# A third early chunk, the last batch's low halves between the two maxima, and a reordered hand-over from attention to the experts

## The reference, cut to what matters

```python
# x: 8 x 512 x 256, context: 8 x 1024 x 256, 8 heads of 64, 8 experts, d_ff 1024, top-2
x = x + tanh(g_xattn) * (softmax(q k^T * 64**-0.5) v @ Wo + bo)     # q from layernorm(x), k and v from context
h = layernorm(x).reshape(4096, 256)
probs = softmax(h @ router.T); topk_probs, selected = top_k(probs, 2)   # weights normalised to sum 1
# each expert takes at most capacity = 1280 (token, weight) pairs, heaviest first
# weights are normalised again per token over what was kept
pre, gate = h_e @ W1_e.T, h_e @ Wg_e.T
out[token] += kept_weight * ((pre * silu(gate)) @ W2_e.T)
x = x + tanh(g_ffn) * out
```

## Time and profile before

| | |
|---|---|
| median of 3 runs | 1765.65 us (1765.6 to 1765.99) |
| the profiled execution | 1766.5 us, its span 1764.8 us |
| busy share | PE 95%, DVE 72%, ACT 60%, POOL 39% |
| chain that ended last | PE 79%, DVE 9%, issue 4%, POOL 3%, ACT 2% |
| attention | to about 1085 us |
| hand-over (END, two early chunks) | about 1085 to 1149 us |
| regular chunks of the experts | 1149 us to the end |

### The profile page before, as it was taken

The page is one execution under the profiler, slowest core; times in us unless marked ns, Lnnn a source line. Parts: engine busy times, 40 slices in busy tenths (PEclk is TensorE's granted clock), DMA queues, the critical chain, the costliest instruction groups (busy, mean ns, idle before and its releaser), DMA issues.

```text
span 1764.8 us, 35399 instructions
## 1 busy us (share of the span) xinstructions
PE 1683.3 (95%) x13198; PEld 1534.2 (87%) x13198; DVE 1268.9 (72%) x2664; ACT 1055.9 (60%) x2233; POOL 688.4 (39%) x622
## 2 busy tenths in 40 slices
PE   6999999999999999999999987899999999999998
PEld 5778888888888888888888876899999999999998
DVE  6888888888888888888888876665465555645443
ACT  5767667667667667767767765354454444545443
POOL 3342444444444444444444335234232323333323
PEclk9999999999999999999999998999999999999999
DMA  4300210210210210210200223232331313131111
GB/s 123 122 25 1 109 49 26 110 48 26 110 48 25 111 48 25 112 47 25 112 35 25 112 82 104 72 101 41 102 103 31 102 31 102 34 99 31 30 30 25
DMA packets 60040, 114.40 MB, mean 65 GB/s; under 512 B 7032, under 2 KB 47992, under 8 KB 59264
## 3 DMA queue, kind: packets, MB, share of 16 engines
q1 hardware_dynamic: 43856, 93.50, 14.9%
q0 software_dynamic: 16048, 19.09, 6.1%
HBM read 88.67 MB, written 57.97 MB: 83 GB/s over the span
## 4 chain that ended last, share of the span: by engine, by line
PE 79%; DVE 9%; issue 4%; POOL 3%; ACT 2%; DMA 1%; POOLq 0%; DVEq 0%; SPq 0%
PE ffn L1020 11%; PE ffn L1022 11%; PE ffn L1021 11%; PE ring L1163 11%; PE turned L1057 11%; PE scores L1045 9%; DVE neg_max L1765 4%; PE ring L1020 4%; PE ring L1022 3%; PE ring L1021 3%; DVE pt_l L1542 2%; PE ring L1129 1%; PE ring L1131 1%; POOL lists L841 1%; POOL probs L866 1%
## 5 line engine op out<-in xcount | busy, mean ns | idle before, releaser
L866 POOL TENSOR_SCALAR probs<-probs,row_rec 128x1024 f32<-128x1024 f32 x256 | 285.4, 1128 | 477.3 <-DVE row_rec L1844 464.1
L1337 ACT ACTIVATE pt_h<-turned 128x512 fp32r<-128x512 f32 x512 | 280.1, 603 | 208.2 <-PE turned L1057 207.9
L1542 DVE TENSOR_TENSOR pt_l<-turned,pt_h 128x512 fp32r<-128x512 f32 x512 | 331.5, 681 | 6.7 <-ACT pt_h L1337 5.7
L1765 DVE TENSOR_REDUCE neg_max<-scores 128x1 f32<-128x1024 f32 x256 | 301.3, 1218 | 36.8 <-PE scores L1045 36.8
L1057 PE MATMUL turned<-ident,probs 128*128 128x128 f32 x2048 | 281.9, 279 | 31.6 <-DVE pt_l L1542 24.4
L1057 PEld LDWEIGHTS turned<-ident,probs 128*128 128x128 f32 x2048 | 223.3, 141 | 100.7 <-issue 72.0
L1393 ACT ACTIVATE probs<-scores,neg_max 128x1024 f32<-128x1024 f32 x256 | 285.4, 1117 | 10.4 <-DVE neg_max L1765 10.4
L1163 PE MATMUL ring<-pt_h,v_hl 128*128 128x256 f32 x1024 | 262.9, 294 | 0.2
L2059 DVE TENSOR_TENSOR act_f<-ffn,silu 128x256 f32<-128x256 f32 x288 | 122.2, 424 | 191.0 <-ACT silu L1489 184.9
L1489 ACT ACTIVATE silu<-ffn 128x256 f32<-128x256 f32 x288 | 110.7, 384 | 237.6 <-PE ffn L1022 225.1
L1163 PE MATMUL ring<-pt_l,v_hl 128*128 128x256 f32 x1024 | 252.3, 284 | 0.0
(11 more groups left out here) (239 smaller groups left out, 4073.7 us busy)
## 6 DMA issues: line engine op xcount, KB each, us to landing
lists<-pads SPq DMA_DIRECT2D x8, 4160.0 KB
w_raw<-w_t SPq DMA_DIRECT2D x14, 1024.0 KB, 6.3
e_rows<-lists SPq DMA_DIRECT2D x37, 260.0 KB
ctx_raw<-ctx_t SPq DMA_DIRECT2D x15, 512.0 KB, 3.7
wg_raw<-wg_t SPq DMA_DIRECT2D x7, 1024.0 KB
x_in<-x SPq DMA_DIRECT2D x8, 512.0 KB, 4.0
x_sum<-x SPq DMA_DIRECT2D x8, 512.0 KB, 3.9
out<-x_sum SPq DMA_DIRECT2D x8, 512.0 KB, 2.9
```

Of the source, the lines that this page charges most:

```text
L866: nc.gpsimd.tensor_scalar(probs[:, k, :], probs[:, k, :], row_rec[:, k:k + 1], 1.0, ALU.mult, ALU.mult).then_inc(scaled, 1)
L1337: return nc.scalar.activation(dst, src, ACT.Copy)
L1542: return nc.vector.tensor_tensor(dst, src, hi_part.bitcast(F32), ALU.subtract)
L1765: nc.vector.tensor_reduce(neg_max[:, k:k + 1], scores[:, n % 2, :].rearrange("p (a c) -> p a c", a=2), AX.XY, ALU.max, negate=True).then_i ...
```

## The change

1. `EARLY` is 3: expert 0's third chunk, too, is written out as an early chunk, with its result in `y_early`. An expert's chunks after the early ones are at least `LEAST_MORE` = 2, so expert 0 has at least five. Each early chunk transposes the next chunk's rows at its part 6, and takes the high and low halves of them at part 7.
2. `closing` has another order: END 0 and 1, the rows of chunk 0, END 2 and 3, then the early chunks with the other END steps behind named parts. The projections ("w", 1, 2) and ("w", 1, 3) are now behind part 0. The search is spread over parts 0 to 8 of early chunk 2.
3. In the last batch at steps 24 to 30 DVE takes the low halves of unit u - 2 between the maxima of u and u + 1. The reciprocals of the last two units are apart, and POOL scales each when it is there. "r" of batch 6 is at step 25, its DVE part after both maxima of step 26; POOL scatters two by two at steps 27 to 30.
4. ACT's six high pieces are at LAST 23, 25, 27, 29 and END 3, 4. POOL's low pieces, ten, are all at END 0, in the order 0, 2, 4, 6, 1, 3, 5, 7, 8, 9, behind its wait for the scatters; DVE takes pieces 10 and 11 at END 8. PE waits for 4, 8, 9, 10, 11, 12 pieces where it needs them.
5. SP waits for the scatters itself; POOL stores the kept weights in one DMA. POOL adds the early chunks one by one, each within the first chunk of expert 1, 2 and 3, between `gather` and `scatter_add`.

```diff
-EARLY = 2
+EARLY = 3
+LEAST_MORE = 2
...
-LAST_STEPS_OF = {("k", 3, 0): 17, ("k", 3, 1): 18}
+LAST_STEPS_OF = {("k", 3, 0): 17, ("k", 3, 1): 18, ("r", 0, 0): 25}
...
+LAST_HIGHS = {23: 0, 25: 1, 27: 2, 29: 3}
+END_HIGHS = {3: 4, 4: 5}
+FIRST_LOWS = [0, 2, 4, 6, 1, 3, 5, 7, 8, 9]
+SECOND_LOWS = [10, 11]
+LOW_BETWEEN = (24, 26, 28, 30)
...
+            chain = {
+                (0, 0): (4, 5, 6, 7, 8), (0, 1): (9, 10), (0, 2): (11,), (0, 4): (12, 13), (0, 5): (14, 15),
+                (0, 6): (16,), (0, 7): (17, 18), (1, 0): (19,), (1, 1): (20,), (1, 2): (21,), (1, 4): (22, 23),
+                (1, 5): (24,), (1, 6): (25,), (1, 7): (26,)}
...
+            steps(0, 1)
             rows_of(0)
-            steps(3, 4, 5, 6, 7, 8)
-            both(0, 0)
-            steps(9, 10, 11)
-            both(0, 1)
-            both(0, 2)
-            both(0, 3)
-            steps(12, 13)
-            up_part(0, 4)
-            steps(14)
-            down_part(0, 4)
-            steps(15)
-            up_part(0, 5)
-            steps(16)
-            down_part(0, 5)
-            steps(17, 18, 19)
-            both(0, 6)
-            steps(20, 21)
-            both(0, 7)
-            steps(22, 23)
-            early_end(0)
-            both(1, 0)
-            steps(24)
-            both(1, 1)
-            steps(25, 26)
-            both(1, 2)
-            search(0)
-            for c in range(3, 8):
-                both(1, c)
-                search(c - 2)
-            early_end(1)
-            search(6)
-            rows_of(2)
+            steps(2, 3)
+            for g in range(EARLY):
+                for c in range(FC):
+                    up_part(g, c)
+                    down_part(g, c)
+                    steps(*chain.get((g, c), ()))
+                    if g == EARLY - 1:
+                        search(c)
+                early_end(g)
+            search(FC)
...
@@ gpsimd
+                    if body is END and u == 0:
+
+                        for n in (UNITS - 2, UNITS - 1):
+                            k = n % 4
+                            pool.wait_ge(rec_done, UNITS // 2 * B + n - UNITS + 2)
+                            alone(pool)
+                            nc.gpsimd.tensor_scalar(probs[:, k, :], probs[:, k, :],
+                                                    row_rec[:, k:k + 1], 1.0,
+                                                    ALU.mult, ALU.mult).then_inc(scaled, 1)
+                    elif u % 2 == 0 and (body.own if u > 0 else body.prev):
...
-                    if body is LAST and u in (24, 26, 28):
-                        for p in {24: (0, 1), 26: (2, 3, 4), 28: (5, 6)}[u]:
-                            low_first(p)
                     if body is END and u == 0:
-                        for p in range(7, PIECES):
+
+                        pool.wait_ge(listed, 16 * 2 * QT * (B - 1))
+                        for p in FIRST_LOWS:
...
+                        if body is LAST and u in range(27, 31):
+                            for k in range(2):
+                                scatter(b - 1, 2 * (u - 27) + k)
+                        if u == UNITS - 1 and body is not LAST:
...
+            pool.wait_ge(fw_done, 1)
+            nc.gpsimd.dma_start(weights_of[0:E * T, :].rearrange("(p k) o -> p (k o)", k=GT),
+                                by_expert[:, :]).then_inc(fw_stored, 16)
+            pool.wait_ge(fw_stored, 16)
...
+            expert(0)
+            for e in range(1, 1 + EARLY):
+                chunks = pool.value_load(table[0:1, 0, ds(e, 1)], min_val=LEAST_MORE,
+                                         max_val=T // CHUNK)
+                before = pool.value_load(table[0:1, 1, ds(e, 1)], min_val=0,
+                                         max_val=MOST_CHUNKS)
+                g = pool.snap(before + 0)
+                gather(g)
+                pool.wait_ge(added, g * (16 * ST) + 16 * ST)
+                alone(pool)
+                gather_early(e - 1)
+                add_early(e - 1)
+                pool.wait_ge(early_added, 16 * ST * e)
+                scatter_add(g)
+                with pool.Fori(1, chunks) as j:
+                    g = pool.snap(before + j)
+                    gather(g)
+                    scatter_add(g)
+            with pool.Fori(1 + EARLY, E) as e:
...
@@ tensor
-                    pe.wait_ge(w_split, PIECES)
+                    pe.wait_ge(w_split, PER_WEIGHT)
 
                     pe.wait_ge(exp_done, UNITS * B)
+                if g == 0 and c == FC // 2:
+                    pe.wait_ge(w_split, 2 * PER_WEIGHT)
...
+                if g == 0 and c >= BEHIND and (c - BEHIND) % 2 == 0:
+                    pe.wait_ge(w_split, 2 * PER_WEIGHT + (c - BEHIND) // 2 + 1)
...
@@ vector
+                    lows = body is LAST and u in LOW_BETWEEN + (UNITS - 1,)
+                    late = [(what, c) for what, c in jobs if lows and what[0] == "r"]
+                    jobs = [job for job in jobs if job not in late]
...
+                        if lows:
+                            low_turned(b, u - 2, 0)
+                            low_turned(b, u - 2, 1)
+                        if body is LAST and u == UNITS - 2:
+
+                            k = u % 4
+                            v.wait_ge(exp_done, at(b, UNITS, u + 1))
+                            nc.vector.reciprocal(row_rec[:, k:k + 1], row_sum[:, k:k + 1])\
+                                .then_inc(rec_done, 1)
                         highest(b, u + 1)
+                    for what, c in late:
+                        drain(body, u - 1, what, c)
                     between(body, u, 1)
+                    if body is LAST and u == UNITS - 1:
+                        for j in range(2):
+                            low_turned(b, u - 2, j)
                     if body.own and u % 2 == 1:
 
...
+                    if body is END and u == 8:
+
+                        v.wait_ge(w_split, len(FIRST_LOWS))
+                        alone(v)
+                        for p in SECOND_LOWS:
+                            low_first(p)
...
+                part = {0: 0, 1: 1, 3: 2, 4: 3, 6: 4, 8: 6}.get(slot)
...
-                    own(nc.vector.tensor_scalar(table_f[:, 0, 0:1], table_f[:, 0, 0:1], float(EARLY), None,
-                                                ALU.subtract))
+                    own(nc.vector.tensor_scalar(table[:, 0, 0:1], table[:, 0, 0:1],
+                                                float(EARLY + LEAST_MORE), float(EARLY),
+                                                ALU.max, ALU.subtract))
+                    own(nc.vector.tensor_scalar(table_f[:, 0, 0:1], table_f[:, 0, 0:1],
+                                                float(EARLY + LEAST_MORE), float(EARLY),
+                                                ALU.max, ALU.subtract))
```

More of the change, by code:

```diff
@@ L1194, in _, with search @@
             batches(pe, run)
[L1197 removed]
+            def search(slot):
+                part = {1: 1, 4: 3, 6: 4, 8: 5}.get(slot)
                 if part == 1:
@@ L1420, in step @@
                             .then_inc(gate_exp, 1)
-                    if body is LAST and u in range(22, 28):
-                        i, half = (u - 22) // 2, (u - 22) % 2
+                    n = LAST_HIGHS.get(u) if body is LAST else END_HIGHS.get(u) if body is END else None
+                    if n is not None:
+                        i, half = n // 2, n % 2
                         cols = slice(half * 2 * PIECE, (half + 1) * 2 * PIECE)
@@ L1848, in step @@
                     between(body, u, 2)
-                    if body.prev if u < 2 else body.own:
+                    if (body.prev if u < 2 else body.own) and not lows:
                         low_turned(b, u - 2, 0)
```

105 lines of the change are left out of this document (47 added, 58 removed).

## The result

The changed kernel takes 1759.31 us (median of 6 runs, 1757.54 to 1760.77), the kernel before 1765.84 (6 runs, 1765.6 to 1766.8). The ratio is 0.996, 95% interval 0.995 to 0.9971: 6.5 us faster, where 15 were forecast. The profiled execution took 1759.72 us with a span of 1758.0; 6.8 us of span are gained. The time lies at the upper end of the range.

The account below looks back on a forecast made before the run. PE was taken as the bound, busy 95%, with time winnable only in its waits in slices 24 to 26. 11.1 + 0.1 + 3.1 + 2.1 - 1.0 = 15.4 us saved; forecast 1750.5 us, own range 1746 to 1755, wider range 1743 to 1760.

Parts of the forecast that it names:

- What bounds the kernel, and the floor of work: Whole kernel: PE busy 95%, time winnable only in slices 24 to 26; five chunks in expert 0, floor unchanged.
- The last batch: Step 22 to chunk 0's first `up`: 59.35 us becomes 48.25, 11.1 saved, of which 1.9 come back in chunk 0.
- the sign I had set (below 3): PE's wait for low halves: falling from 8.7 us below 3 would show the forecast right.
- The weights ... I take 0 between 0 and 3.5: POOL's ten and DVE's two low pieces around chunk 0: cost PE nothing, with 1.5 us to spare; range 0 to 3.5.
- Chunk 0: Expert 0's first chunk: 23.02 us becomes 22.9, projections adding 1.9, clock and ranks taking time off.
- rival 2: Hand-over: POOL's scatters and ten pieces become the bound, steps 28 and 30 at 10.5 and 19, DVE held; 1754 to 1760, 20%.
- Chunks 1 and 2: Expert 0's next two chunks: 46.73 us becomes 43.6 (18.6 and 25.0), 3.1 saved; the search wait of 2.2 stays.
- The early adds ... I take 0.5 in all: Experts 1 to 3: gather ahead of the adds saves 2.6 us, late adds cost 0.5, so 2.1 saved.
- Rival 3: Experts 1 to 3: slow indirect steps land the chunk's add 8 us later, PE loses 15 us; 1765 to 1771, 6%.
- Code, 1.0: Third early chunk's straight-line code: one more PE wait for "issue", 1.0 us added, between 0 and 2.6.
- rival 1: Last batch and chunk 2: clock never falls, search hidden, no code wait; 1744.5 us, 17%.
- the missing wait for y: Expert 1: no wait for y there would show the forecast right.

Follow-up runs that it names:

- e4: Changed kernel with the last batch's low halves at steps 24, 26 and 28 behind both maxima again; ratio to the kernel before 0.9919.
- e6: Changed kernel with four of POOL's ten low pieces moved back into the last batch, at steps 24 and 26; ratio to the kernel before 0.9916.
- e2: Changed kernel with POOL adding the early chunk before it gathers the chunk's weights in experts 1 to 3; ratio to the kernel before 0.9919.
- t0_again: The changed kernel run once more with no edit; ratio to the kernel before 0.995.
- e1: Changed kernel with all three early adds put back together in expert 1, ahead of POOL's loop; ratio to the kernel before 0.9946.
- c2_scat: Changed kernel, early adds before gather, four low pieces at steps 24 and 26, DVE's two at END 12, scatters at 28 to 31; ratio to kernel before 0.9877.
- c7_best5: c2_scat once more, in five rounds, without a further edit; 1747.4 us against 1767.22 for the kernel before on that chip.

## Why the prediction was wrong, step by step

- **What bounds the kernel, and the floor of work**: right. Five chunks in expert 0, and all gains and losses are waits and the clock behind them.
- **The last batch**: right as a sum, 48.9 for 48.25, and in part by luck: 2.8 us too much in steps 24 and 28 stand against 2.1 too little in the others. Steps 22, 26 and 30 came within 0.1, 0.4 and 1.7 of 6.6, 7.75 and 17.3. Step 24 took 7.8 for 7.0; of step 28's bounds, 8.7 to 10.5 without and with the lower clock, even the upper was passed (11.5). The scaling did hold the turn, 2.6 as forecast 2.7, but the third scores then waited 1.7 for an exponential, which I had not followed. Its cause was credited wrongly: I gave 3.5 us of step 24 to the low halves between the maxima, less 0.7 in step 26. e4 shows 1.6 there, and 1.4 to 2.5 lost in step 28. PE's waits for low halves fell from 8.7 to 3.0, at the edge of the sign I had set (below 3).
- **"The weights ... I take 0 between 0 and 3.5"**: this step failed. Chunk 0 took 26.67 for 22.9, 3.8 more. I let DVE start its two pieces when the tenth of GpSimd's was there, 5.6 us into the chunk. It started them 9.0 in: 6.6 in even without a hold (e6), since its own work for the layernorm stands in front, 7.7 with one piece's hold and 9.0 with two. The second low half was ready 11.6 us in, not 8.4, and PE, which asked for it 10.1 in, waited. The hold of one operation was 2.4 us, where I had seen 1.1. And my price was too low: 0.5 for 2 us of hold left out the wait for `rows` and the lower clock. By the rule of the Trainium skill (GPSIMD Engine Reference, Specifications), which I had in rival 2, the operation with two SBUF inputs contends with GpSimd's; the trace agrees, 2.83 us against 0.43. Rival 2, at 20%, was right in DVE's hold and in step 28 (11.5 for 10.5), not in step 30 (15.7 for 19). That the time lies in its 1754 to 1760 is luck in part, since it had neither the price of the adds nor the end.
- **Chunks 1 and 2**: right, 17.9 + 24.5 for 18.6 + 25.0. The search wait stays and varies between 1.7 and 3.3. The number owes something to the execution: thirteen of the sixteen other profiles of this kernel and its edits have 2.1 to 3.4 us less.
- **"The early adds ... I take 0.5 in all"**: this step failed. Experts 1 to 3 lost 0.5 where I had 2.1 saved. I had the timing right (the chunk's own add 24.5 us in; 25.6 measured) and DVE's late part too, up to 4 us (5.4 at most), but not the price: 4.9 us, by e2. The chunk's gather in front, which I had put ahead as a gain, waits 7.39 us for `y_at` and holds all that stands behind it. I let DVE be 4 us late before PE is, but 3.7 and 4.0 cost PE 1.0 and 1.2, and 5.4 cost 2.8. Rival 3 named this place; its 15 us did not come.
- **Code, 1.0**: wrong and harmless. The longest wait for `issue`, which I read as code, is 0.5 in the early chunks; that of 1.3 in the earlier trace rows is not there in the new order.
- **The end**: in no step. 3.2 us lie behind the last instruction of DVE, a place that I did not open because the change does nothing there. The share view before did show it: the last of the 40 slices, too, was below nine tenths (8), and it is at 7 after.
- **"Every lower-clock stretch in rows 1 follows a wait of over 2 us"**, the argument for rival 1: not so. The one that lies across the rows with 0.98 and 0.95 follows a wait of 1.9, and in the changed kernel the one in chunk 0 follows waits of 1.5 and 1.6.

Of the 8.6 us between forecast and span, 3.8 are chunk 0, 2.6 the early adds, 3.2 the drain and 0.6 and 0.9 the last batch and the rest of expert 0; chunks 1 and 2 with the code give 2.3 back, and experts 4 to 7 and the start 0.2. Of the signs, the late start of chunk 3 (1155.7, not near 1153) and DVE's wait of over 4 us in a second chunk said wrong; the first `up` at 1086.7 and the missing wait for y said right. The steps at fault were undone: with chunk 0 and the adds mended the kernel takes 1747.4, which is 19.8 faster than before on the same chip, beyond the forecast even with the long drain. Part of that is luck: in that version's profile chunks 1 and 2 gained 6.7, not 3.1.

## What to carry to other kernels

- When work is moved to a helper engine in one queue, ask of each of its instructions what it waits for, and put ahead those that wait for nothing: putting one gather behind the early adds was worth 4.9 us over three experts.
- When an engine has only one or two microseconds to spare in front of the bottleneck, price the contention by the helper's instruction, not by the longest hold seen so far: a hold of 1.1 was on record, and with pieces of 1.3 us it became 1.1 or 2.4. Count the lower clock behind it (0.9 here).
- An edit that shortens the step under the eye may only move the wait; time it over the whole stage. Twice here (lows between the maxima, later scatters) a step lost 1.6 and 3.1 us and the stage nothing.
- Profile the unchanged kernel a second time before an edit is credited: t0_again took 1.3 us less in chunk 0 and e1, with the same code up to there, 2.2, of the 3.3 that e6 seemed to save.

## What the runs showed of the hardware that was not expected

- GpSimd's closing drain took 5.6 to 5.7 or 8.5 to 9.0 us. It goes with where the early chunks' indirect adds stand, some 400 to 540 us earlier (four profiles with them together, fourteen with them in three places), and not with the code's length or loops as far as they were varied. The mechanism is open.
- A DVE operation with two SBUF inputs, 128x256, took 0.43 us when GpSimd's `tensor_tensor` pieces were over and 1.54 to 1.57 or 2.80 to 2.83 beside them, in the same place of the program. It ended 0.3 us after the end of the first or of the second piece: waiting did not give it the next turn.
- The same search loop of PE and DVE made PE wait 1.7 or 3.2 us, in code that does not differ in these two engines; among the changed kernel and its edits nothing lay between.
- TensorE's lower clock came or did not come behind the same waits (t0_again and e1 in chunk 0, c2_scat and c7_best5 in chunk 2), and cost 0.9 and 1.3 us.
